# Scatters of a batch's routed rows, four and four, at the head of its first and second group on GpSimd

## What is computed

```python
def _L0_attn_ref(hidden_states, ...):
    q = shape_heads((hidden_states @ wq.T + bq) * scaling)
    k = shape_heads(hidden_states @ wk.T + bk)
    v = shape_heads(hidden_states @ wv.T + bv)
    scores = jnp.einsum('bhtd,bhsd->bhts', q, k)
    mask = jnp.triu(jnp.full((T, T), -10000.0, dtype=jnp.float32), k=1)
    attn = jax.nn.softmax(scores.astype(jnp.float32) + mask, axis=-1).astype(jnp.float16)
    out = jnp.einsum('bhts,bhsd->bhtd', attn, v)
    return out.transpose(0, 2, 1, 3).reshape(B, T, E) @ wo.T + bo

def _L0_ffn_ref(x, Ws, bs, Wg, Wu, Wd):          # per row: the 2 best of 8 experts
    topk_w, topk_idx = jax.lax.top_k(xt @ Ws + bs, K)
    combine = jnp.sum(jax.nn.one_hot(topk_idx, E) * softmax(topk_w)[..., None], axis=1)
    h = jax.nn.silu(xt @ Wg[e]) * (xt @ Wu[e])
    out = sum over e of (h @ Wd[e]) * combine[:, e]

x = x + _layernorm(attention(_layernorm(x)))
x = x + _layernorm(experts(_layernorm(x)))
```

## Time and profile before

| | |
|---|---|
| time, median of 3 runs (lowest to highest) | 892.8 us (891.81 to 897.83) |
| the profiled execution: its own time, its span | 890.5 us, 888.7 us |
| PE busy | 718.2 us, 81% of the span |
| DVE busy | 635.0 us, 71% |
| ACT busy | 536.3 us, 60% |
| POOL busy | 434.0 us, 49% |
| the 64 scatters of L162 | 66.9 us of POOL |
| the 128 instructions of L728 | 88.2 us of POOL |
| mean granted clock of PE | 0.908 |

### The profile page before, as it was taken

The page is one execution under the profiler, slowest core; times in us unless marked ns, Lnnn a source line. Parts: engine busy times, 40 slices in busy tenths (PEclk is TensorE's granted clock), DMA queues, the critical chain, the costliest instruction groups (busy, mean ns, idle before and its releaser), DMA issues. The chain is left out here.

```text
span 888.7 us, 22060 instructions
## 1 busy us (share of the span) xinstructions
PE 718.2 (81%) x6822; PEld 471.2 (53%) x6823; DVE 635.0 (71%) x2034; ACT 536.3 (60%) x1086; POOL 434.0 (49%) x515
## 2 busy tenths in 40 slices
PE   3476787778788899979998998889885999999930
PEld 1144444445443355545554564567773878778720
DVE  5777898889877988887897778467551556556545
ACT  4688875867656676756765674665642444344427
POOL 3563432644534556774675467577352233242228
PEclk9889997989985799999988997899996999999975
DMA  6435232463332101221112111223335233233248
GB/s 192 136 118 153 82 113 71 126 194 116 112 130 63 43 14 26 50 48 26 26 28 53 19 32 34 41 40 57 50 86 137 37 44 46 36 47 42 30 113 291
DMA packets 72812, 68.91 MB, mean 78 GB/s; under 512 B 6800, under 2 KB 66320, under 8 KB 72720
## 3 DMA queue, kind: packets, MB, share of 16 engines
q1 hardware_dynamic: 59440, 53.23, 19.7%
q0 software_dynamic: 13280, 14.49, 11.6%
HBM read 34.04 MB, written 31.29 MB: 74 GB/s over the span
## 5 line engine op out<-in xcount | busy, mean ns | idle before, releaser
L944 ACT ACTIVATE pT<-bank 128x512 f16<-128x512 f32 (+1 forms) x384 | 200.3, 534 | 100.1 <-PE bank L1521 98.7
L728 POOL TENSOR_SCALAR_AFFINE_SELECT pT<-pT 128x512 f16<-128x512 f16 x128 | 88.2, 734 | 144.7 <-ACT pT L944 144.4
L1087 DVE TENSOR_REDUCE nmax<-bank 128x1 f16<-128x384 f32 (+2 forms) x216 | 126.1, 597 | 34.7 <-PE bank L1510 33.3
L1944 POOL DMA_INDIRECT expert_rows<-y_sb,dest x36 | 56.0, 1554 | 120.1 <-DVE y_sb L2063 114.6
L1100 DVE CUSTOM_DVE_ANT_0 unused<-bank,mask 128x384 f16<-128x384 f32 (+2 forms) x224 | 103.6, 483 | 14.4 <-PE bank L1499 12.8
L2138 PE MATMUL bank<-xT,gu_part 128*128 128x256 f16 (+1 forms) x792 | 95.9, 280 | 2.6 <-issue 1.7
L1614 PE MATMUL bank<-tile_xT,gu_part 128*128 128x256 f16 (+1 forms) x616 | 90.9, 289 | 8.5 <-DVE stage L1284 8.4
L2138 PEld LDWEIGHTS bank<-xT,gu_part 128*128 (+1 forms) x792 | 78.5, 102 | 19.0 <-issue 4.2
L1552 PEld LDWEIGHTS bank<-va,pT 128*128 128x128 f16 x1280 | 55.4, 99 | 51.1 <-issue 27.8
L1552 PE MATMUL bank<-va,pT 128*128 128x17 f16 x1280 | 68.0, 174 | 15.8 <-POOL pT L728 15.8
L162 POOL DMA_INDIRECT dispatch_rows<-rows,slot x64 | 66.9, 1046 | 21.5 <-issue 16.7
(11 more groups left out here) (218 smaller groups left out, 1618.6 us busy)
## 6 DMA issues: line engine op xcount, KB each, us to landing
expert_rows<-tile_in SPq DMA_DIRECT2D x8, 1024.0 KB, 6.2
stage<-wg SPq DMA_DIRECT2D x8, 688.0 KB, 4.2
stage<-wu SPq DMA_DIRECT2D x8, 688.0 KB, 4.2
stage<-wd SPq DMA_DIRECT2D x8, 640.0 KB, 4.3
gu_part<-expert_rows SPq DMA_DIRECT2D x16, 256.0 KB, 5.7
out<-gu_part SPq DMA_DIRECT2D x16, 256.0 KB, 2.9
tile_in<-dispatch_rows SPq DMA_DIRECT2D x21, 130.0 KB, 2.2
rows<-dispatch_rows SPq DMA_DIRECT2D x18, 130.0 KB, 2.2
```

The lines of the kernel that those rows point to most:

```text
L728: last = gp.affine_select(out=diagonal, in_=diagonal, compare_op=ALU.is_ge, fill=0.0, base=0, pattern=[[0, J], [1, P]], channel_multiplier=-1)
L944: sc.activation(pT[:, lo:hi], ST_BANK[i % 2][:, 0:hi - lo], ACT.Exp, scale=1.0 / INV_SCALE).then_inc(p_ready, 1)
L1087: v.tensor_reduce(columns, S_BANK[i % 2][:, 0:n * len(heads)].rearrange("p (j n) -> p j n", n=n), AX.X, ALU.max, negate=True).then_inc(s_m ...
```

## The change

The table `AT_SCATTER` goes. In POOL's `batch(b)`, from b = 2 on, four of the eight scatters are issued at the head of group 0, ahead of everything else of that group, and four at the head of group 1. The wait for `slot_ready` and `copy_ready` moves with the first four. The scatters behind the last batch (outside `batch`) stay as they are.

```diff
-        AT_SCATTER = ((0, 1), (0, 2), (1, 0), (1, 2))
+        SCATTER_IN = (0, 1)
...
                     for g in range(G):
+                        if g in SCATTER_IN and scattering:
+                            if g == SCATTER_IN[0]:
+                                pool.wait_ge(slot_ready, b - 1)
+                                pool.wait_ge(copy_ready, b - 1)
+                            scatter_rows(gp, keep, xs_dram, SCATTER_IN.index(g), len(SCATTER_IN))
                         for c in range(CUTS):
                             at = (g, c)
                             if at == (0, 0) and not in_last:
...
-                            if at in AT_SCATTER and scattering:
-                                if at == AT_SCATTER[0]:
-                                    pool.wait_ge(slot_ready, b - 1)
-                                    pool.wait_ge(copy_ready, b - 1)
-                                scatter_rows(gp, keep, xs_dram, AT_SCATTER.index(at), len(AT_SCATTER))
```

## The result

The changed kernel takes 917.44 us (median of 4 runs, 913.97 to 918.04) beside 892.3 us for the kernel before: a ratio of 1.0252, 95% interval 1.0205 to 1.0298. It is slower, by some 25 us, where I had said 893.1 us and at most 898. Three later measurements, each on a chip of its own, gave ratios of 1.0302, 1.0293 and 1.028. The profiled execution took 917.0 us with a span of 915.2 us and a mean granted clock of 0.888.

A forecast was written before the change was run, and what follows sets the result against it. DVE is busiest up to 264 us, PE from 340 to 590 us; POOL counts only where its results come late. Gains of 3.6 us and losses of 3.9 us gave +0.3 us: 893.1 us on the median, range 888 to 898.

The forecast's parts named there:

- What is added at a batch head: Batch heads: slot wait and four scatters ahead of the rsqrt delay DVE's scaling by 2.3 us in batches 2 and 3.
- The sum of these losses: Late rsqrt at the heads of batches 2 and 3: 1.5 + 2.4 = 3.9 us lost, bounds 2 to 8.9 us.
- PE's waits for masks: Sign in the profile after: falling from 15.8 to about 10 us, with none in groups 21, 25 and 29.
- I take 1.8 us each for groups 21 and 25: Two scatters gone ahead of cut 1 there: gain 1.8 us per group, of PE's 1.95 us wait.
- the hold of DVE that I gave to group 29 alone: Group 29: DVE's L1245 held 2 us by POOL's back-to-back instructions, so the gain there is 0.
- rival 3: DVE is held in groups 21 and 25 too, both gains go: 896.7 us; chance 0.15, including one group only.
- I cost them at nothing: Four scatters at the head of group 1 fall into a pause of POOL before the next group's cut 0: 0 us.
- the same delay is hidden: Late rsqrt costs nothing: batch 4 through DVE's 3.82 us idle, batch 5 through 1.1 us slack, batch 6 likewise.
- its rivals: Gains only (0.2), long scatters (0.1), DVE held in groups 21 and 25 (0.15), slots ready too late (no separate chance).
- could hide all of this: Closing caveat: a shift of PE's granted clock in one of the stretches could mask the expected signs; no size given.
- 8 in 100 for slower: Chance of 0.08 given to a slowdown beyond about 1%, 8.9 us; same 0.88, faster 0.04.

The follow-up runs named there:

- the run with b < 5: Changed kernel's four and four scatters only in batches 2 to 4, later batches as in the kernel before; 899.88 us, ratio 1.0034.
- the paired kernel: Against the changed kernel, two scatters at the head and two behind cut 1 of groups 0 and 1 each; 896.45 us, ratio 1.005.

## Why the prediction was wrong

**Right.** "What is added at a batch head": the rsqrt late by 2.3 us, DVE standing for it in batches 2 and 3, hidden in batches 5 and 6. Measured 2.22 and 2.00 us (and 1.81 us in batch 4, where I had looked only at what comes behind); scatters of 0.95 to 1.25 us at that place, where I took 1.0. The sum of these losses, 3.9 us, against 1.2 + 4.4 us on one chip and 3 us in the run with b < 5. On chip P batches 2 to 4 lost more, so the number has some luck in it. PE's waits for masks, forecast at about 10 us, fell to 8.5.

**Wrong in size: "I take 1.8 us each for groups 21 and 25".** The mask stalls are gone, but the hold of DVE that I gave to group 29 alone came in all three: L1245 took 2.12, 1.15 and 1.61 us, and PE stands 1.17 us for L1284 in group 21. That was rival 3, and the pair moved one cut on (ratio 1.0025) shows it too: nothing is gained by taking these stalls away. This is 3.6 us at most.

**Wrong in kind: "I cost them at nothing".** This sentence on the four scatters at the head of group 1 is the step that failed, and the four at the heads of batches 5 and 6, "the same delay is hidden", with it. I looked only at POOL's time. For that the sentence holds: 5 us of power operations in that place give 0.9992. But behind four scatters in a row PE's semaphore increments come up to some 3 us late on four of six chips, and ACT, DVE and PE stand for it where POOL's time is covered. The sum has no term for this. All of its rivals were about POOL or DVE being late, and none about a result that is ready and not announced.

**Left out: the clock.** I named a shift of the granted clock as something that "could hide all of this", and gave it no price. PE stood for up to 1.9 us at a time, and ran at 1.2 GHz for a stretch behind the first such stall of batch 5. On chip S 5.4 us more of idle time came with 14.2 us more of busy time, 19.6 us in all. Hence the size: the rivals' terms were added up as plain stalls, with 1% at the top.

**What the profile could have told.** Its tail has the same runs of four without any late increment, since it comes from an execution of the harmless kind. Nothing in it shows the trap. But the scatters were all in pairs up to the tail, and a run of four beside a busy PE was an operation that the trace of before did not show in these batches. I should have bounded it from both sides and held more than 8 in 100 for slower.

**Settled and open.** Shown: on chips that lag, a run of four scatters that GpSimd issues, not POOL's being busy and not the scatters' being early, costs some 20 us in batches 5 to 7; pairs cost nothing. Shown: late increments come with it on some chips and not on others, with the same program. Not shown: what holds the increments, why the chip matters, and how much of the 25 us a chip without the lag would show; on chip P kernels with four in a row lost 8 and 15 us with no late increment at all.

A rival is left untested: that the recording itself holds them back. On the chips that lag, the trace lacks the record of 10 to 22 of the 384 increments that DVE makes behind its maxima, and every one that is missing falls while GpSimd issues indirect DMAs or within 1.3 us behind; on P, on T and in my profile of before none is missing. Lag and lost records come together, and no run on record tells which of them makes the other, if either does. The link from stall to clock rests on where a low stretch lies, and on the split of one pair of runs; a stall alone, without anything else changed, was not tried.

## What to carry to other kernels

Indirect DMAs that GpSimd issues are not only its own time: put no more than two of them in a row while other engines are exchanging results every microsecond, and let GpSimd's own compute work stand between the pairs. Where PE sets the pace, a new stall can cost the clock behind it as well; here new idle time of 5.4 us came with 3.6 times as much in all. When the waits name nobody, look at when the increments were posted, and profile the kernel before and after on one chip. The absence of such a row does not say that nothing was late: compare when the waiting engine takes up the same result.

## What the runs showed of the hardware

- PE's semaphore increments queue up behind four scatters in a row and are then posted some 0.05 us apart (eleven from 375.23 to 375.71), the first 3.3 us late, 0.81 us after the fourth scatter's end; behind six in a row ACT stood 4.15 us, behind a pair 1.21 to 1.27 us on chips Q and S. Late increments of other engines than PE I did not find in group 21. The Trainium skill says of the SBUF ports "PE and ACT never wait on anyone" ("SBUF — State Buffer", section "Who interferes with whom"); PE's matmuls did run on, so the trace does not speak against it, but what others learn of PE came late.
- Chips differ: four of six lagged (Q, R, S, U), and so did the chip of the first result, two did not (P, T), and the kernel before takes the same time on both kinds to 0.5% (medians of 891.4 and 891.7 us on P and T, 892.3 to 895.6 on the others, where S shows the lags in its tail). A trap of this kind does not show in the time of a kernel that has stepped around it.
- A DVE addition of 128x8 with two SBUF inputs was held for 2.98 us through three back-to-back instructions of POOL; the same hold in the paired kernel (2.99 us) cost next to nothing.
- Stalls of 4.8 and 5.6 us behind late increments in the tail hardly change the time: from the last L1217 on it takes 243.0 us without and 243.5 us with them. The stretch ahead of it, with one of 5.2 us, takes 59.6 instead of 57.7 us.
